# Cross-attention and gated FFN on one core: the context given a second time, keys last, and a new layout of slots

## The reference

```python
h = layernorm(x)
q, k, v = h @ Wq, ctx @ Wk, ctx @ Wv            # split into 16 heads
a = softmax(q k^T / 8) v                        # per head; keys 1444
x = x + tanh(g_xattn) * (a @ Wo + bo)
z = layernorm(x)
hid = silu(fp4(z) @ fp4(w_gate).T) * (fp4(z) @ fp4(w_up).T)
x = x + tanh(g_ffn) * (fp4(hid) @ fp4(w_down).T)
```

## Time and profile before

| | us |
|---|---|
| median of three timed runs | 571.11 |
| lowest, highest | 570.98, 574.01 |
| the profiled execution | 572.5 |
| its span in the trace | 570.7 |
| TensorE busy | 534.2 (94%) |
| VectorE busy | 433.4 (76%) |
| ScalarE busy | 311.2 (55%) |
| GpSimd busy | 272.2 (48%) |

### The profile page before, as it was taken

The page is one execution under the profiler, slowest core; times in us unless marked ns, Lnnn a source line. Parts: engine busy times, 40 slices in busy tenths (PEclk is TensorE's granted clock), DMA queues, the critical chain, the costliest instruction groups (busy, mean ns, idle before and its releaser), DMA issues.

```text
span 570.7 us, 8404 instructions
## 1 busy us (share of the span) xinstructions
PE 534.2 (94%) x2841; PEld 333.0 (58%) x2841; DVE 433.4 (76%) x769; ACT 311.2 (55%) x731; POOL 272.2 (48%) x251
## 2 busy tenths in 40 slices
PE   5779999999999999999999999999999999999832
PEld 4555565666656565656566565656566565656421
DVE  2768876779786887779796887779787887776745
ACT  3444564666565754566565755566565755546411
POOL 4007427292735456292735456282735365284700
PEclk9789999999999999999999999999999999999975
DMA  8600000300011000300021000300020000000000
GB/s 154 114 1 0 2 1 0 57 2 1 1 38 23 1 1 1 61 0 1 0 48 15 0 1 1 61 1 0 2 56 1 1 2 0 5 1 2 4 1 4
DMA packets 27898, 9.45 MB, mean 17 GB/s; under 512 B 24016, under 2 KB 27600, under 8 KB 27856
## 3 DMA queue, kind: packets, MB, share of 16 engines
q1 hardware_dynamic: 27856, 8.92, 8.5%
HBM read 8.50 MB, written 0.41 MB: 16 GB/s over the span
## 4 chain that ended last, share of the span: by engine, by line
PE 82%; DVE 10%; issue 3%; ACT 3%; POOL 1%; DMA 1%; SPq 0%; POOLq 0%; ACTq 0%; DVEq 0%
PE attn L807 24%; PE scores L793 16%; PE ring L746 12%; PE scores L794 11%; PE ring L760 5%; PE ring L753 4%; DVE max L915 3%; PE ring L725 3%; PE ring L732 2%; DVE acc_v L935 2%; PE ring L766 2%; ACT q_hh L583 1%; PE ring L774 1%; PE ring L749 1%; DMA x_in<-in_x 1%
## 5 line engine op out<-in xcount | busy, mean ns | idle before, releaser
L648 ACT ACTIVATE probs<-scores 120x400 f32<-120x400 f32 (+1 forms) x384 | 186.5, 504 | 193.0 <-PE scores L794 190.2
L915 DVE TENSOR_REDUCE max<-ring 116x1 f32<-116x482 f32 (+1 forms) x336 | 205.1, 653 | 57.7 <-PE ring L746 54.2
L513 POOL TENSOR_TENSOR acc_p<-acc_p,probs 120x800 f32<-120x800 f32 x79 | 152.7, 1934 | 71.7 <-ACT probs L648 65.8
L807 PE MATMUL attn<-probs,ctx_n 120*64 120x400 f32 (+1 forms) x768 | 171.8, 526 | 0.0
L793 PE MATMUL scores<-q_hh,k_hl 128*120 128x400 f32 (+1 forms) x384 | 153.5, 400 | 1.2 <-DVE q_ls L917 1.2
L793 PEld LDWEIGHTS scores<-q_hh,k_hl 128*120 128x120 f32 (+1 forms) x384 | 70.2, 183 | 125.6 <-ACT probs L648 72.0
L794 PE MATMUL scores<-q_ls,k_h 71*120 71x400 f32 (+1 forms) x384 | 133.9, 349 | 0.0
L746 PE MATMUL ring<-k_hl,q_hh 128*116 128x482 f32 (+1 forms) x336 | 119.5, 411 | 5.7 <-DVE k_hl L911 2.3
L794 PEld LDWEIGHTS scores<-q_ls,k_h 71*120 71x120 f32 (+1 forms) x384 | 70.9, 185 | 4.2
L746 PEld LDWEIGHTS ring<-k_hl,q_hh 128*116 128x116 f32 (+1 forms) x336 | 58.2, 182 | 16.6 <-DVE max L915 7.0
L807 PEld LDWEIGHTS attn<-probs,ctx_n 120*64 120x64 f32 (+1 forms) x768 | 38.1, 135 | 46.4 <-issue 34.4
(11 more groups left out here) (129 smaller groups left out, 484.2 us busy)
## 6 DMA issues: line engine op xcount, KB each, us to landing
ctx_n<-in_ctx SPq DMA_DIRECT2D x16, 360.0 KB
wq<-in_L_xattn_Wq SPq DMA_DIRECT2D x1, 512.0 KB, 4.6
wo<-in_L_xattn_Wo SPq DMA_DIRECT2D x1, 512.0 KB, 7.2
x_in<-in_x SPq DMA_DIRECT2D x8, 50.0 KB
out<-y_out SPq DMA_DIRECT2D x8, 50.0 KB
wk<-in_L_xattn_Wk SPq DMA_DIRECT2D x1, 256.0 KB, 3.8
ctx_n<-in_ctx SPq DMA_DIRECT2D x16, 1.0 KB
wv<-in_L_xattn_Wv SPq DMA_DIRECT2D x1, 256.0 KB, 6.2
```

The source lines that it names most:

```text
L513: pool.tensor_tensor(acc_p[0:r, t.g % 2, :], left, probs[0:r, c % PROBS, :], ALU.add).then_inc(sum_p, 1)
L648: act.activation(probs[0:r, c % PROBS, k * HALF:(k + 1) * HALF], scores[0:r, slot % SCORE_BANKS, 0:HALF], ACT.Exp).then_inc(probs_full, 1)
L807: mm = pe.matmul(attn[64 * i:64 * i + C, k, 0:HALF], ctx_n[0:r, par, c, 0, :], probs[0:r, c % PROBS, k * HALF:(k + 1) * HALF], start=(j == ...
L915: dve.tensor_reduce(max3[0:rows, tile, part:part + 1], src[0:rows, 0:MAXC[part + 1] - MAXC[part]], AX.X, ALU.max).then_inc(free, 1)
```

## The change

The host gives the context a second time, transposed (64 rows, keys last, in the order of the chunks), and Wq, Wk and Wv transposed. The 12 context transposes of a batch, the transposes of the weights and their copies out of the ring are gone. `ctxT` (one buffer, 64 x 1444) is loaded per batch, behind waits for the copies of the one before; ScalarE copies halves of 722 columns from it to `k_hl` and `k_h1` at slots of their own, and VectorE subtracts `ctxT` minus `k_hl` (`split_k`, L905 of the changed file) at slots 15 and 22. `ctx_n` holds the context once. P.V pairs stand at slots given by `PV_SLOTS` and no longer at every second one; the scaling of heads, the q copies and splits, the attention copies and several steps of GpSimd have slot tables of their own; and the tables of the ring users, of the layer norms and of the quantization steps have new numbers, partly one set for even and one for odd groups.

```diff
-MAX_SLOTS = {1: 1, 2: 1, 4: 1, 5: 2, 7: 3, 8: 2, 10: 2, 11: 2, 12: 1, 13: 2, 14: 1, 15: 1, 16: 1, 17: 1}
-FFN_SLOTS = {2: ('zT', 0), 4: ('gate', 0), 6: ('up', 0)}
-DOWN_SLOTS = {2: ('hT', 0), 3: ('hT', 1), 5: ('down', 0)}
+MAX_SLOTS = [{1: 1, 3: 1, 4: 1, 5: 3, 7: 1, 8: 1, 9: 2, 10: 2, 11: 2, 13: 1, 14: 3, 15: 2, 16: 1}, {2: 2, 5: 1, 6: 1, 7: 3, 8: 2, 10: 3, 11: 2, 12: 1, 13: 2, 14: 1, 15: 1, 16: 2}]
+MAX_TILES_SLOT = [16, 16]
+SHIFT_SLOT = [21, 19]
+FFN_SLOTS = {1: ('zT', 0), 4: ('gate', 0), 6: ('up', 0)}
+DOWN_SLOTS = {1: ('hT', 0), 2: ('hT', 1), 3: ('down', 0)}
 LAST_FFN_SLOTS = {**FFN_SLOTS, 19: ('hT', 0), 20: ('hT', 1), 22: ('down', 0)}
-W_SLOTS = {slot: ("wT", i) for i, slot in enumerate(LAST_FFN_SLOTS)}
-POST_SLOTS = {6: ('sum', 0), 8: ('proj', 0), 10: ('proj', 1)}
-CTX_SLOTS = {14: ('ctx', 0), 15: ('ctx', 1), 18: ('ctx', 2)}
-XT_SLOT = 20
-MAX_TILES_SLOT = 17
-SHIFT_SLOT = 20
-
-
-LN2_SLOTS = [12, 13]
-LN2_APPLY_SLOT = 17
-Z_SLOTS = [19, 19, 20, 21, 21, 21, 22, 22, 22]
+W_SLOTS = {slot: ("wT", i) for i, slot in enumerate((2, 4, 6, 19, 20, 22))}
+POST_SLOTS = [{5: ('sum', 0), 6: ('proj', 0), 10: ('proj', 1)}, {6: ('sum', 0), 8: ('proj', 0), 10: ('proj', 1)}]
+XT_SLOT = 10
+LN2_SLOTS = [13, 14]
+LN2_APPLY_SLOT = 19
+Z_SLOTS = [16, 16, 16, 19, 19, 19, 21, 21, 21]
 SIGMOID_SLOTS = [5, 6]
-H_SLOTS = [18, 19, 19, 20, 21, 21, 22, 22, 23]
+H_SLOTS = [17, 17, 17, 17, 17, 19, 20, 21, 23]
 LAST_H_SLOTS = [7, 8, 9, 10, 11, 12, 13, 14, 16]
-ADD_LAG, LAST_ADD_SLOT = 3, 0
+ADD_LAG, LAST_ADD_SLOT, ADD_LAST_SLOT = 3, 0, 1
+PV_SLOTS = [5, 6, 8, 10, 10, 14, 18, 19, 21, 22, 24, 24]
+COPY_SLOTS = [3, 5]
+Q_SLOT = 0
+Q_COPY_SLOTS = [0, 0, 0, 0]
+Q_LO_SLOTS = [0, 0]
+HEAD_SLOTS = [7, 7, 8, 8, 9, 10, 10, 10]
+LN1_SLOTS = [2, 3, 7]
+CTX_COPY_SLOTS = [13, 16, 17, 20]
+K_LO_SLOTS = [15, 22]
+POOL_AT = {'ln1': 1, 'ln2': 7, 'swiglu': (0, 2, 4), 'heads': 5}
...
-START = [("wkT", 0), ("wqT", 0), ("xT", 0), ("A", 0), ("ctx", 0), ("q", 0), ("ctx", 1)]
-BETWEEN = {1: ('ctx', 2), 4: ('wqT', 1), 7: ('A', 1), 9: ('wvT', 0), 13: ('vo', 0), 14: ('vo', 1), 16: ('vo', 2), 20: ('vo', 3)}
+START = [("xT", 0), ("A", 0), ("q", 0), ("A", 1)]
+BETWEEN = {8: ('vo', 0), 11: ('vo', 1), 14: ('vo', 2), 17: ('vo', 3)}
...
-            sp.dma_start(wk[:, :], Wk).then_inc(wk_in, 16)
-            sp.dma_start(wq[:, :], Wq).then_inc(wq_in, 16)
+            def load_qk(k):
+                heads = slice(4 * k, 4 * k + 4)
+                for r in range(2):
+                    rows = slice(64 * r, 64 * r + C)
+                    sp.dma_start(wkT[rows, heads, r, :], WkT[rows, heads, :]).then_inc(qk_in[k], 16)
+                sp.dma_start(wqT[:, heads, :], WqT[:, heads, :]).then_inc(qk_in[k], 16)
+
             load_x(0, 0)
-            load_ctx(0, 0)
+            load_qk(0)
+            sp.dma_start(ctxT[:, :], ctxT_in[0, :, :]).then_inc(ctxT_loaded, 16)
             sp.dma_start(tanh_x[:, :], g_xattn.partition_broadcast(128)).then_inc(small_in, 16)
             sp.dma_start(tanh_f[:, :], g_ffn.partition_broadcast(128)).then_inc(small_in, 16)
             sp.dma_start(bo_bc[:, :], bo.partition_broadcast(128)).then_inc(small_in, 16)
-            sp.dma_start(wv[:, :], Wv).then_inc(wvo_in, 16)
+            load_qk(1)
+            load_ctx(0, 0)
+            for i in range(2):
+                sp.dma_start(wvT[:, :, i, :], WvT).then_inc(wvo_in, 16)
             sp.dma_start(wo[:, :, :], Wo.rearrange("(j p) n -> p j n", p=128)).then_inc(wvo_in, 16)
...
                     load_x(t.batch(1), t.parity(1))
+                    sp.wait_ge(k_hi_done, 4 * t.batch(1))
+                    sp.wait_ge(k_lo_done, 2 * t.batch(1))
+                    sp.dma_start(ctxT[:, :], ctxT_in[t.batch(1), :, :]).then_inc(ctxT_loaded, 16)
...
+            def copy_k(t, step):
+
+                part, par = step // 2, t.parity(1)
+                cols = slice(KC[part], KC[part + 1])
+                if step == 0:
+                    act.wait_ge(ctxT_loaded, 16 * t.batch(2))
+                act.activation((k_hl, k_h1)[step % 2][par][0:C, cols], ctxT[:, cols], ACT.Copy).then_inc(k_hi_done, 1)
...
-                elif kind == "ctx":
-                    a, b = COFF[4 * k], COFF[4 * k + 4]
-                    par = t.parity(1)
-                    if t.g >= 0:
-                        act.activation(k_h1[par][0:C, a:b], src[0:C, 0:b - a], ACT.Copy)
-                    act.activation(k_hl[par][:, a:b], src[:, 0:b - a], ACT.Copy).then_inc(k_hi_done, 1)
...
+                    for step in [i for i in range(4) if Q_COPY_SLOTS[i] == slot and t.g + 1 < GROUPS]:
+                        copy_q(t, step)
+                    for step in [i for i in range(4) if CTX_COPY_SLOTS[i] == slot and t.g % 2 == 0 and t.g + 2 < GROUPS]:
+                        copy_k(t, step)
+                    for h in [i for i in range(HG) if HEAD_SLOTS[i] == slot and t.g >= 1]:
+                        scale_head(t, h)
...
-                elif kind == "ctx":
-                    par = t.parity(1)
-                    if k == 0:
-                        pe.wait_ge(ctx_loaded[par], 64 * t.fills(1))
-                    for c in range(4 * k, 4 * k + 4):
-                        r, a = CROWS[c], COFF[c] - COFF[4 * k]
-                        mm = pe.transpose(dst[:, a:a + r], ctx_n[0:r, par, c, :, :].rearrange("p i d -> p (i d)"), ident[0:r, 0:r])
...
+                if i == 0 and t.g % 2 == 0:
+                    pe.wait_ge(ctx_loaded[par], 32 * t.fills())
...
-                    if slot % 2 == 0:
-                        i = slot // 2 - 2
-                        if i >= 0:
+                    for i in range(CHUNKS):
+                        if PV_SLOTS[i] == slot + SLOTS and t.g >= 1:
+                            attn_pair(t, i, 1)
+                    for i in range(CHUNKS):
+                        if PV_SLOTS[i] == slot:
                             attn_pair(t, i, 0)
-                        elif t.g >= 1:
-                            attn_pair(t, i + CHUNKS, 1)
...
+            def split_k(t, part):
+
+                par = t.parity(1)
+                cols = slice(KC[part], KC[part + 1])
+                dve.wait_ge(k_hi_done, 4 * t.batch(1) + (part + 1 if t.g < 0 else 2 * part + 1))
+                dve.tensor_tensor(k_hl[par][C:128, cols], ctxT[:, cols], k_hl[par][0:C, cols].bitcast(F32), ALU.subtract).then_inc(k_lo_done, 1)
...
+def laid_out(np, inputs):
+
+    keys = np.concatenate([np.arange(c, c + CHUNKS * PFULL, CHUNKS) if c >= EXTRA else np.append(np.arange(c, c + CHUNKS * PFULL, CHUNKS), CHUNKS * PFULL + c)
+                           for c in range(CHUNKS)])
+    views = {name: inputs[name] for name in _INS}
+    views["ctxT"] = inputs["ctx_512"][:, keys, :].transpose(0, 2, 1)
+    for name in ("Wq", "Wk", "Wv"):
+        w = inputs["L0_xattn_" + name]
+        views[name + "T"] = w.T.reshape(HG, 128, w.shape[0]).transpose(1, 0, 2)
+    return {name: np.ascontiguousarray(a) for name, a in views.items()}
```

209 lines of the change are left out of this document (98 added, 111 removed).

## The result

The changed kernel takes **591.39 us** (median of four runs, 588.49 to 595.48) against 571.71 us before (570.98 to 574.01): ratio 1.034, 95% interval 1.026 to 1.043. It is slower, as forecast (577.5), but by 19.7 us instead of some 6, and outside the range of 558 to 584. The profiled execution took 595.5 us (span 593.5), 23 more than that of before.

The account below looks back on a forecast made before the run. TensorE was taken as the bound, VectorE as possibly late next. Even groups 4 to 12 +7.0, group 2 +1.2, group 14 +2.0, group 1 -0.7, last -0.3, start -3.3: +5.9, forecast 577.5 us, range 558 to 584.

Parts of the forecast that it names:

- The hold by GpSimd's adds and the z wait: Even groups from 2 on: z steps wait out GpSimd's adds ahead of the shift, so TensorE waits 2.2 us.
- The even group's number: Steady even groups 4 to 12: 34.0 us against 32.60, +1.4 each, +7.0 for five.
- the early waits: Even groups' early slots: h transpose 0.55, down product 0.6, row sum without cover; of 1.3 us about 0.9 extra.
- The split's part: Even groups: the context split of two SBUF tensors waits between GpSimd's adds, 0.9 of the 2.2 us wait.
- Transposes, 1.26 us an even group: Each even group but the last: three sets of context transposes go, saving 1.26 us each, 7.6 for groups 2 to 12.
- P.V pairs, 0.35 a meeting: Pairs back to back at slots 10 and 0: 0.35 us saved per meeting, 0.70 a group, up to 10.5; lower bound 0.
- The odd groups, 0: Odd groups 3 to 13: 31.2 against 31.3 us, as 0.5 lost to the h wait eats most of 0.7 won.
- The start, -3.3: Before the first score: reduces start at 14.6, 0.61 each, ending at 30.8 to 31; 3.3 us won, between 0 and 6.
- Group 0, 0 within 2: Group 0 with the weight quantization: loses transposes but gains collisions; taken as 0, between -2 and +2.
- Group 2, +1.2: Group 2, which has no down product: +1.2 us.

Follow-up runs that it names:

- the old tables: Changed kernel's transposed inputs and start, with every slot table as before the change, context copies at 14 and 18, splits at 15 and 19: 581.10 us (1.015).
- all tables fitted: Changed kernel with context copies at 5 and 6, splits at 7, later z and h steps behind the shift, z transpose at slot 2: 576.33 us.
- the gaps filled: Changed kernel with 28 extra identity transposes on TensorE in the start, 12 ahead of q and 16 ahead of the third maximum: 586.80 us.
- the second profiled execution: Changed kernel run again with no edit: 593.08 us over six executions, profiled span 591.5.
- The old tables there: Changed kernel with the slot tables from before the change in group 0 alone, nothing filled in: 589.20 us.
- the run of 576.5 us: Transposed inputs with slot tables from before the change, but context copies at slots 5 and 6 and both context splits at 7: 576.51 us (1.007).

## Why the prediction was wrong

By its own steps:

- **The hold by GpSimd's adds and the z wait: right.** The wait was 1.56 of idle time for a forecast 2.2, even groups +1.1 to +1.2 where the clock held, for +1.4. Putting the steps back took it away, at once. The Trainium skill's rule (SBUF — State Buffer, the section on the two separate sides) agrees with the traces: beside a GpSimd add only steps with two SBUF inputs or of a tensor and a scalar were held, while the shift took 1.00 and a reduce of the maxima 0.65 beside an add and without one.
- **The even group's number: close in part by luck.** TensorE's busy time in it fell by 0.7 us (31.67 for 32.39) where the sum had 1.96 (1.26 + 0.70), and its idle time grew by 1.9 (2.06 for 0.21) where the sum had some 3.1 (2.2 + 0.9): of the early waits only 0.35 for the down product came. Two errors of like size gave 33.7 for 34.0.
- **The split's part: right in kind, 0.6 us for 0.9.** With the old tables it costs more than the transposes give: 64.6 a pair for 63.8.
- **Transposes, 1.26 us an even group: a quarter too much.** With the splits out of the way the even group gains 0.9.
- **P.V pairs, 0.35 a meeting: too much.** Two together take 1.49 for 2 x 0.82, which is 0.15. The rows beside a lone pair were taken as caused by it; that gap stays with whatever stands there. With all tables fitted (31.4 and 30.6 against 31.7 and 31.2) pairs and the rest of the new slots bring 0.45 a group. Alone they lose.
- **The odd groups, 0: right where the clock holds** (31.3), but a wait for the shift can be followed by a piece at half clock, 1.1 to 1.4 us more, and in three odd groups it was: +4.4. The prediction gave a wait its own length and nothing behind it.
- **The start, -3.3: this step failed.** It was +1.5. The first reduce came at 14.87 for a forecast 14.6. Then 0.61 a reduce was taken, VectorE's own pace (those terms add up to 30.6 and not to 30.8 to 31, which changes nothing here). TensorE ran at 1.2 GHz, three maxima and a V.O set took 3.49, and the last reduce ended at 35.3. The earlier trace rows had the reduces of before beside products at full pace; transposes stood among them there, and the change removes them. With the gaps filled the last reduce ended at 28.3, and the first score came at 30.5 for 33. That the half pace is the cost is shown by that run; that the missing transposes brought it about is likely and not shown. The Trainium skill has this (TensorE: Matmul & The Clock Gate, Part 1, on the clock gate): the array is at 1.2 GHz by default and after idling, at 2.4 GHz once kept busy. The filled start agrees (1.11 us for the eight q products that took 2.00). The unfilled one agrees only in part: TensorE had no break from 17.2 to 34.1 us, and stayed at 0.50 up to 48.6. I had not weighed the clock at all.
- **Group 0, 0 within 2: this step failed.** +5.2, and +2.4 in the second profiled execution. The old tables there give 4.3 and 1.5 of it back. I had named the collisions with the weights' quantization and not counted them: the scalar step L354 took 1.79 us for 0.19 before, the layer norm's L898 1.49 for 0.34, TensorE waited 2.03 for a maximum at 62.77 and ran at half clock up to 72.5. Where no half clock followed the wait, the group was 1.8 over before (33.9), within the range; the rest is the clock.
- **Group 2, +1.2:** +1.9 without the half-paced piece (33.2), +5.0 with it. The row sum moved to slot 5 waits 0.93 there, as said of the later groups; in group 2, without a down product, TensorE comes sooner. What starts the fall just there was not settled.

So direction and mechanism of the steady part held. The 14 us missing (17 in the profiled execution) lie in the start (4.8 over the forecast), group 0 (5.2), group 2 (3.8) and the odd groups (4.4), less 1.3 elsewhere: waits in the stages that aren't steady, and half clock in the start and behind some of the waits. What decides whether a wait is followed by half clock stays open.

## What to carry to other kernels

Taking work off the bounding engine is worth what the next engine lets through: here the same transposed input, under the old tables, gave +0.8 us a pair of groups with the splits at slots 15 and 19, beside GpSimd's adds, and -0.9 with both at slot 7. A VectorE step of two SBUF inputs is to be placed by GpSimd's timeline, in its idle stretch, before any table around it is tuned. A gap on TensorE must be priced with the half-paced stretch that can follow it, and transposes that keep it busy in the start may be worth more than the time they take.

## What was not expected of the hardware

- The granted clock's column can miss a half-paced stretch: in the run of 576.5 us it read 1.00 from 22 to 36 us while sets of eight V.O products took 2.07 (1.16 at full pace). That trace holds no record of the clock before 47 us. Durations of a known product are the surer sign. The Trainium skill warns (TensorE: Matmul & The Clock Gate, Part 1) that the clock's trace events are unreliable; these rows agree.
- 51 extra transposes in the start, on the engine that bounds the kernel, made it 8.6 us faster; 46 in the start of the kernel before made it some 1.7 faster.
